# A decoder layer on one core: sums of squares moved from VectorE to adding DMAs, a named table set for Gelu, a new order on every engine

## The reference

```
re, im  = num_re / den, num_im / den
mean_sq = (sum(re**2) + sum(im**2)) / (2 * H * M)      # over the 8 x 4 values of a head
rs      = rsqrt(mean_sq + 1e-5)
y       = (re * rs * norm_re) @ W_re + (im * rs * norm_im) @ W_im
out     = (y * silu(gate)) @ out_proj
```

## Time and profile before

| | us |
|---|---|
| median of 3 runs | 1030.68 (1026.15 to 1031.63) |
| the profiled execution, own time | 1032.04 |
| its span, first to last instruction | 1030.3 |
| busy TensorE, VectorE, ScalarE, GpSimd | 911.1, 792.5, 565.7, 44.7 |
| mean granted TensorE clock | 0.963 of full speed |

### The profile page before, as it was taken

The page is one execution under the profiler, slowest core; times in us unless marked ns, Lnnn a source line. Parts: engine busy times, 40 slices in busy tenths (PEclk is TensorE's granted clock), DMA queues, the critical chain, the costliest instruction groups (busy, mean ns, idle before and its releaser), DMA issues.

```text
span 1030.3 us, 11040 instructions
## 1 busy us (share of the span) xinstructions
PE 911.1 (88%) x3719; PEld 553.9 (54%) x3738; DVE 792.5 (77%) x1301; ACT 565.7 (55%) x902; POOL 44.7 (4%) x112
## 2 busy tenths in 40 slices
PE   0489945889999999989998999989999999999795
PEld 0145623555575647654766457644766476647345
DVE  3778799778987899779987799779988997183141
ACT  0566674487428564767457553885467745421410
POOL 0000100100001000100010000100010002000000
PEclk9889986999999999999998999999999999999899
DMA  5900100010002000110001000200002000000000
GB/s 153 239 1 1 62 0 0 21 42 1 1 14 69 1 1 1 43 41 1 1 21 61 1 1 1 83 1 0 1 1 62 1 1 21 1 0 1 21 1 21
DMA packets 39082, 25.48 MB, mean 25 GB/s; under 512 B 18647, under 2 KB 38642, under 8 KB 39026
## 3 DMA queue, kind: packets, MB, share of 16 engines
q1 hardware_dynamic: 39026, 24.77, 8.6%
HBM read 20.57 MB, written 4.19 MB: 24 GB/s over the span
## 4 chain that ended last, share of the span: by engine, by line
PE 64%; DVE 15%; ACT 13%; issue 5%; SPq 1%; POOL 1%; DMA 0%; ACTq 0%; DVEq 0%; POOLq 0%
PE ps L811 9%; PE ps L792 9%; PE ps L783 9%; PE ps L672 7%; PE ps L610 4%; PE ps L595 3%; PE ps L640 3%; PE ps L716 3%; PE ps L463 3%; PE ps L656 3%; DVE zc L2460 2%; PE ps L726 2%; DVE sc L2539 2%; ACT x L1674 2%; ACT L1422 1%
## 5 line engine op out<-in xcount | busy, mean ns | idle before, releaser
L2539 DVE TENSOR_TENSOR_SCAN sc<-mask,sc 128x1024 f32<-128x1024 bf16 x64 | 146.3, 2285 | 0.5
L783 PE MATMUL ps<-cum,mw 128*128 128x512 f32 x256 | 121.9, 598 | 3.2 <-ACT cs L1669 2.9
L792 PE MATMUL ps<-x2t,mv 128*128 128x512 f32 x256 | 121.6, 597 | 1.6 <-DVE prod L2767 0.7
L811 PE MATMUL ps<-up,prod 128*128 128x256 f32 x512 | 116.2, 380 | 1.3 <-DVE prod L2767 0.9
L811 PEld LDWEIGHTS ps<-up,prod 128*128 128x128 f32 x512 | 95.1, 190 | 15.9 <-issue 3.8
L1669 ACT ACTIVATE cs<-ps 128x512 f32<-128x512 f32 x64 | 37.9, 592 | 102.4 <-PE ps L783 98.1
L2460 DVE SCALAR_TENSOR_TENSOR zc<-ps,cw,zc 128x510 f32<-128x510 f32 (+2 forms) x96 | 71.3, 743 | 22.7 <-ACT zc L1484 20.3
L2531 DVE TENSOR_TENSOR sc<-sc,g 128x1024 f32<-128x1024 f32 x64 | 77.7, 1214 | 9.7 <-ACT sc L1555 9.6
L1573 ACT ACTIVATE sq<-sc 128x1024 f32<-128x1024 f32 x48 | 50.4, 1050 | 58.7 <-DVE acc L2551 58.7
L783 PEld LDWEIGHTS ps<-cum,mw 128*128 128x128 f32 x256 | 47.3, 190 | 58.8 <-issue 56.2
L595 PE MATMUL ps<-xt,win 128*128 128x512 f32 x128 | 66.7, 650 | 9.5 <-DVE zc L2460 9.5
(11 more groups left out here) (263 smaller groups left out, 1551.6 us busy)
## 6 DMA issues: line engine op xcount, KB each, us to landing
xa<-in_x_dram SPq DMA_DIRECT2D x8, 512.0 KB, 3.5
xs_a<-in_x_dram SPq DMA_DIRECT2D x8, 512.0 KB, 3.8
cin<-in_ctx_dram SPq DMA_DIRECT2D x8, 512.0 KB, 5.6
out_dram<-prod SPq DMA_DIRECT2D x8, 512.0 KB, 4.8
prod<-in_L_ffn_V_fwd_dram SPq DMA_DIRECT2D x2, 256.0 KB
prod<-in_L_ffn_W_fwd_dram SPq DMA_DIRECT2D x2, 256.0 KB
prod<-in_L_ffn_W_inv_exp_dram SPq DMA_DIRECT2D x2, 256.0 KB
prod<-in_L_ffn_V_inv_dram SPq DMA_DIRECT2D x2, 256.0 KB
```

What stands on the lines that cost most here:

```text
L783: last = mm(o, mw[:, t, br, c:c + P], cum[:, t, :], start=(t == 0), stop=(t == 1))
L792: last = mm(o, mv[:, t, br, c:c + P], x2t[:, t, :], start=(t == 0), stop=(t == 1))
L811: mm(d, prod[:, j, q * P:(q + 1) * P], up[:, j, :], start=(j == 0), stop=False)
L2539: V.tensor_tensor_scan(flat, mask[:, 0:2 * T], flat, 0.0, ALU.mult, ALU.add)\
```

## The change

1. a_accumulate leaves VectorE. GpSimd issues a DMA with an adding destination in its place, 6 per chunk, 48 in all, each 128x1024 floats from sq[h] to acc[h], counted by a semaphore for each half. VectorE keeps the two half sums (a_both) and waits there for the third add of its half. ScalarE's squares wait for the DMA before, where they waited for VectorE's add.
2. c_hidden asks for a third set, GELU. ScalarE's list has 54 changes of set now.
3. The lists of all engines and of SP are new. biases() stands behind a_scan(0, 7) instead of ahead of a_moments(0, 2); the split of the bias row on GpSimd (bias_parts) stands behind rstd of b(0). At the end of a chunk VectorE does the residuals of b(i-1) and c(i-2) mostly between a_scan(i, 7) and a_both(i, .). In VectorE's list of the middle chunks the products of c stand ahead of units 2 to 7 of a. PE has b_transform(i, "cf") between a_squares(i) and its two a_factor, and transposes of c between those of a.

```diff
-EXP_LN, SILU_SIN = "natural_log_exp_and_others", "silu_and_others"
+EXP_LN, SILU_SIN, GELU = "natural_log_exp_and_others", "silu_and_others", "gelu_and_others"
...
+        added = [sem(f"pool_a_add{h}") for h in range(2)]
...
             load_x(1)
+            load_ctx(1)
+            load_residual(1)
             load_x(2)
-            load_residual(1)
-            load_ctx(1)
             load_x(3)
             load_residual(2)
             load_ctx(2)
+            store(0)
+            load_residual(3)
             load_x(4)
-            load_residual(3)
-            store(0)
             load_ctx(3)
+            load_ctx(4)
+            store(1)
+            load_residual(4)
             load_x(5)
...
# ScalarE, a_squares
-                    if m > 1:
-                        act.wait_ge(*VEC_A.at(i, "acc", u - 2))
-                    elif not is_first(i):
-                        act.wait_ge(*VEC_A.at(i - 1, "acc", UNITS - 2 + h))
+                    if m > 1 or not is_first(i):
+                        act.wait_ge(added[h], 16 * ((M - 1) * i + m - 1))
...
             def c_hidden(i, n):
-                tables(SILU_SIN)
+                tables(GELU)
...
# GpSimd
+            def a_accumulate(i, u):
+                m, h = divmod(u, 2)
+                pool.wait_ge(*ACT_A.at(i, "sq", u))
+                if m > 1:
+                    pool.wait_ge(added[h], 16 * ((M - 1) * i + m - 1))
+                else:
+                    pool.wait_ge(*ACT_A.at(i, "sq", h))
+                G.dma_start(acc[:, h, :, :], sq[:, h, :, :], accum_op=ALU.add).then_inc(added[h], 16)
+            a_accumulate(0, 2)
...
+            a_accumulate(0, 7)
             rstd(0, 0, VEC_A, POOL_A)
...
             rstd(0, 1, VEC_B, POOL_B)
+            bias_parts()
...
# VectorE
-            def a_accumulate(i, u):
-                m, h = divmod(u, 2)
-                dve.wait_ge(*ACT_A.at(i, "sq", u))
...
-                TT(acc[:, h, :, :], acc[:, h, :, :], sq[:, h, :, :], ALU.add).then_inc(*VEC_A.tick("acc", u))
-                if m == M - 1:
-                    dve.wait_ge(*VEC_A.at(i, "acc", u))
-                    TT(acc[:, h, 0, :], acc[:, h, 0, :], acc[:, h, 1, :], ALU.add).then_inc(*VEC_A.tick("both", h))
+            def a_both(i, h):
+                dve.wait_ge(added[h], 16 * (M - 1) * (i + 1))
+                TT(acc[:, h, 0, :], acc[:, h, 0, :], acc[:, h, 1, :], ALU.add).then_inc(*VEC_A.tick("both", h))
...
# VectorE's list, end of chunk 0 and of chunk 1
-            biases()
             a_moments(0, 2)
...
             a_scan(0, 7)
-            a_accumulate(0, 5)
-            a_accumulate(0, 6)
-            a_accumulate(0, 7)
+            biases()
+            a_both(0, 0)
+            a_both(0, 1)
             a_weight(0)
...
             a_scan(1, 7)
-            a_accumulate(1, 5)
-            a_accumulate(1, 6)
-            a_accumulate(1, 7)
+            b_residual(0, 0)
+            b_residual(0, 1)
+            a_both(1, 0)
+            a_both(1, 1)
             a_weight(1)
-            b_residual(0, 0)
             a_factor(1)
             a_heads(1, 0)
             a_heads(1, 1)
-            b_residual(0, 1)
             a_residual(1, 0)
```

More of the change, by code:

```diff
@@ L95 @@
               + each("p2 g both gf y", range(2)) + each("frac mom scan", range(UNITS))
-              + [("acc", u) for u in range(2, UNITS)] + LAYER_NORM)
+              + [] + LAYER_NORM)
 ACT_A = Steps("act_a", each("xT silu p1", range(2)) + ["zs", "exp", "phigh", "e", "ln", "f", "fhigh"]
@@ L823, in _ @@
             a_project(0, 2)
+            fold(0)
             a_project(0, 3)
-            fold(0)
+            a_sums(0, 0)
             fold(1)
@@ L871, in _ @@
             a_project(1, 0)
+            fold(33)
             a_project(1, 1)
@@ L926, in _ @@
             c_turn(0)
+            a_spread(2, 1)
+            a_project(2, 2)
+            c_own(0, 0)
+            b_spectrum(1, "qa")
+            b_spectrum(1, "qb")
+            b_spectrum(1, "ka")
+            b_spectrum(1, "kb")
+            b_spectrum(1, "va")
+            b_spectrum(1, "vb")
+            c_weights(0)
             a_project(2, 3)
[L928 to L931, removed]
             c_spread(0, 0)
@@ L1731, in _ @@
             a_angles(0, 4)
+            fold(11)
+            fold(12)
             a_turns(0, 6)
@@ L2309, in _, with bias_parts @@
                 G.memset(t, 0.0).then_inc(zeroed, 1)
-            pool.wait_ge(ready, 2)
-            pool.wait_ge(folded, len(FOLD))
-            for n in range(PARTS):
-                if n:
-                    pool.wait_ge(parts, 2 * n - 1)
-                    G.tensor_tensor(bp[:, :], bp[:, :], bp3[:, n - 1, :], ALU.subtract).then_inc(parts, 1)
-                    pool.wait_ge(parts, 2 * n)
-                G.tensor_copy(bp3[:, n, :], bp[:, :]).then_inc(parts, 1)
+            def bias_parts():
+                pool.wait_ge(ready, 2)
+                pool.wait_ge(folded, len(FOLD))
+                for n in range(PARTS):
+                    if n:
+                        pool.wait_ge(parts, 2 * n - 1)
+                        G.tensor_tensor(bp[:, :], bp[:, :], bp3[:, n - 1, :], ALU.subtract).then_inc(parts, 1)
+                        pool.wait_ge(parts, 2 * n)
+                    G.tensor_copy(bp3[:, n, :], bp[:, :]).then_inc(parts, 1)
             @staged
@@ L2335, in _ @@
             rstd(2, 0, VEC_A, POOL_A)
+            a_accumulate(3, 2)
+            a_accumulate(3, 3)
+            a_accumulate(3, 4)
+            a_accumulate(3, 5)
+            a_accumulate(3, 6)
+            a_accumulate(3, 7)
+            rstd(2, 1, VEC_B, POOL_B)
             rstd(1, 2, VEC_C, POOL_C)
-            rstd(2, 1, VEC_B, POOL_B)
             rstd(3, 0, VEC_A, POOL_A)
+            a_accumulate(4, 2)
+            a_accumulate(4, 3)
+            a_accumulate(4, 4)
+            a_accumulate(4, 5)
+            a_accumulate(4, 6)
+            a_accumulate(4, 7)
+            rstd(3, 1, VEC_B, POOL_B)
             rstd(2, 2, VEC_C, POOL_C)
-            rstd(3, 1, VEC_B, POOL_B)
             rstd(4, 0, VEC_A, POOL_A)
+            a_accumulate(5, 2)
+            a_accumulate(5, 3)
+            a_accumulate(5, 4)
+            a_accumulate(5, 5)
+            a_accumulate(5, 6)
+            a_accumulate(5, 7)
             rstd(3, 2, VEC_C, POOL_C)
@@ L2895, in _ @@
             a_fraction(2, 3)
+            c_normalise(0)
             a_scan(2, 1)
             a_conv(2, 2)
-            c_softmax(0)
-            c_normalise(0)
             c_split(0)
-            a_conv(2, 3)
+            b_products(1)
             c_scale(0, 0)
             c_prod(0, 0)
+            b_heads(1)
+            c_scale(0, 1)
+            c_prod(0, 1)
+            b_topk(1)
+            b_weight(1)
+            c_scale(0, 2)
+            c_prod(0, 2)
+            c_scale(0, 3)
+            a_conv(2, 3)
+            c_prod(0, 3)
+            c_scale(0, 4)
+            b_apply(1)
+            c_prod(0, 4)
+            b_mix(1)
+            c_scale(0, 5)
+            c_prod(0, 5)
             a_moments(2, 2)
             a_fraction(2, 4)
-            c_scale(0, 1)
             a_scan(2, 2)
```

1096 lines of the change are left out of this document (532 added, 564 removed).

## The result

The kernel after takes 995.12 us (median of 4 runs, 994.89 to 1000.13) against 1028.81 (4 runs, 1026.15 to 1031.63): a ratio of 0.9684, 95% interval 0.9640 to 0.9727, 33 us. The span of the profiled execution fell from 1030.3 to 993.5. The forecast was 1014, the range began at 1004: the direction was right, the size was not.

A forecast was written before the change was run, and what follows sets the result against it. TensorE was taken to set the pace from 225 to 950 us, its work fixed, so only its idle time could shrink. 1030.3 - 3 - 4 - 10 = 1013.3 of span, say 1014 measured; own range 1004 to 1022, whole range to 1042.

The forecast's parts named there:

- D = 5.9: Time of one adding DMA: 3.5 us plus half again for the second read, plus 0.6 for GpSimd's issue.
- from chunk 2 on D costs nothing: Ends of chunks from 2 on: the add's transfer is hidden, cost nothing; if cover is gone, 3.5 us a chunk.
- The rival of long adds: Adds longer than two scans hold up ScalarE's squares, deciding from 8.5 us; 1050 at 10 us; chance 0.20.
- Chunk 0, -3: End of chunk 0: bias work behind the last scan hides the add, three adds leave; -3 us, between 0 and -4.
- Chunk 1, -4: End of chunk 1: earlier last scan, normaliser near 183.2 against 188.20, residual work ahead; -4 us, between 0 and -9.
- The steady stretch, -10: 225 to 950 us: half of TensorE's waits on ScalarE and VectorE go, less 1.5 new waits; -10, between +5 and -20.
- Tables: ScalarE: 11 fewer table loads, 14.1 us; rival that this fails loses the ScalarE half, 7.3: 1021, chance 0.08.
- SP's and GpSimd's queues: Reordered loads, stores and normaliser steps: costed at nothing; at worst 3.5 us once for SP, 1 us a chunk for GpSimd.
- PE's floor: Rival: steady stretch already at 96.5%, waits only move; only chunks 0 and 1 give, some 4 us: 1028; chance 0.18.
- Ports: Rival: each GpSimd issue holds VectorE 0.2 to 1.0 us, only the tables help: 1026 to 1031, say 1028; chance 0.06.

The follow-up runs named there:

- e14: Kernel after with all 48 adds left out (no VectorE add, no DMA): 996.21 us, ratio 0.9670 to the kernel before.
- e12: Kernel after with one small GpSimd instruction ahead of each add DMA: 1026.96 us, ratio 0.9980 to the kernel before.
- e18: Kernel after with biases() back ahead of unit 2's moments on VectorE: 995.99 us, ratio 0.9669 to the kernel before.
- e13: Kernel before's old order with Gelu's own table and all 48 adds left out (no VectorE add, no DMA): 1019.02 us, ratio 0.9891 to before.
- e1: Kernel before with one edit, c_hidden asking for the Gelu table set: 1024.08 us, ratio 0.994 to before.
- e5: Kernel before with the adds as DMAs and Gelu's own table, in the old order of TensorE, ScalarE and VectorE: 1029.59 us, ratio 1.0003 to before.
- e8: Kernel after with two serial small GpSimd instructions ahead of every add DMA: 1060.38 us, ratio 1.0304 to the kernel before.
- e2: Kernel before in its old order with only the 48 adds moved to DMAs from GpSimd: 1034.33 us, ratio 1.0045 to before.
- e10: Kernel after with SP's loads and stores and two places of GpSimd's normaliser steps in the old order: 996.18 us, ratio 0.9682 to the kernel before.
- e4: Kernel after with the 48 adds back on VectorE, each chunk's last two right ahead of the half sums: 1049.61 us, ratio 1.019 to the kernel before.
- splices: Adds as DMAs, Gelu's table; old order to chunk 4's squares, then new: 1021.32 us; new order to chunk 1's squares, then old: 1024.44 us.

## Why the prediction was wrong

**The adds, D = 5.9.** Measured 4.9 from square to landing (4.6 from the issue's start), nearer the row of 3.5 us, as chosen; GpSimd's 0.86 us at the issue lies within the 4.6. I let 0.6 for it come on top. No run shows the half again that I added for the second read. The term "from chunk 2 on D costs nothing" was right for the new order (e14), and for the right reason only in part: TensorE is busy until then.

**The rival of long adds.** Its mechanism is real, its point was wrong. I counted 28.7 us of room and a start at 8.5; at 6.9 the cost is already 4.0 us a chunk (e12). The error, as I see it, is in the sum: TensorE's lag of 8.0 us and VectorE's lead of 7.2 were added to the scans' 14.9 as if free, but the half sums that end a chunk must be there when TensorE comes, and that lag is what the last transfer uses. My own rows said so: 7.0 + 1.4 = 8.4 against 8.0. Had D been 6.9, 1.0 above my figure and 2.0 above the measured one, the time would have been 1027. So the forecast was nearer to a failure than its 0.20 says; that D came out on the good side was in part luck.

**Chunk 0, -3.** Measured -0.4 at the squares (98.02 to 97.58), and that with three folds left to do behind them. The reason fell as well: the bias move hides nothing (e18). It could not have hidden the add by my own figures: the last add lands 7.0 us after the scan, and biases() takes 5.0.

**Chunk 1, -4.** The squares come 4.3 us earlier in all, and one context transform (16 matmuls, 3.7 us) is done ahead of them besides: about 8 for the two terms' 7. The place was right: idle PE between chunks 0 and 1 is put to use.

**The steady stretch, -10: the step that failed.** Measured -31.5 between the squares of chunks 1 and 7. The prediction said "PE's work is the same before and after, so the span can only shrink by idle PE time", and gave back "half of each" of the waits, because engines were relieved. The runs show this in its place:
- What relief gives was sized about right. With the adds gone altogether in the old order (e13) this stretch takes 664.9 us against 672.3 before, 7.4 less, most of it the tables' (e1: 665.2); the whole kernel gains 11 us. Of the whole time nothing is left once the transfers have to be waited for (e5). TensorE's largest waits stand in all these runs where they were (rows of 3.3, 3.2 and 2.3 us, as before).
- The reorder was the missing term. Without any adds it takes the stretch from 664.9 us (e13) to 641.6 (e14), 23.3 us less, of which 3.7 are a context transform that it does ahead of the stretch, and it covers the transfers besides (after: 640.9). In the prediction it had no term of its own in the steady stretch; it stood there only as one extra matmul. The waits that I had halved for the relief went because of the order.
- The order removed most of the idle time: PE's idle between these milestones is 28.9 before and 9.1 after. Some 4 of the 28.9 (an estimate) are 15 matmuls whose records are missing (L800, 33 of 48): e5, where none is missing, has 24.8.
- TensorE's busy time is not fixed. It fell by 11.7 us between the milestones, and by 12.6 from e5 to after. 3.7 are the context transform done earlier. Some 6 (an estimate) are matmuls at the lower clock: before, TensorE was busy at a granted clock of 0.50 for some 12 us of this stretch, near 194, 225 and 562 us; after, no 5 us of it have a clock below 1.00. What makes the rest is not shown. The slow ones show in one group, of the interval of chunk 5, before and after:

```profile
L672 PE MATMUL ps<-wks,spec 128*128 128x256 f32 x16 | 6.8, 585 | 3.2 <-ACT qkv L1604 3.2
```
```profile
L673 PE MATMUL ps<-wks,spec 128*128 128x256 f32 x16 | 4.0, 385 | 0.2 <-ACT qkv L1603 0.2
```

Busy time of before in the 5 us behind that wait, the clock in the third place from the end:

```profile
560.00:565.00 5.00, 5.00 (x14) 4.03 (x13) 4.93 (x5) 1.49 (x3) 0.00 (x0) 0.50 0.00 0
```

A wait of 3.2 us cost 2.8 more in this group (6.8 us, where it takes 4.0), at a granted clock of 0.50, the lower of TensorE's two levels (1.2 GHz). In e8 the interval grew by 47.0 us over after: 34.2 are idle, 12.8 are busy time.

**Tables.** 54 loads, as walked; worth 6.4 alone, 4.2 in the new order, 4.7 beside the adds (e2 to e5), against a half credit of 7.3 for ScalarE. The mechanism holds: this relief did reach TensorE. It is the smallest part.

**SP's and GpSimd's queues**, costed at nothing: right (e10).

**The other rivals.** PE's floor (1028) is near e5, the old order (1029.6), but in the number only: there chunks 0 and 1 give nothing (squares of chunk 1 at 188.8, 187.1 before), and in after it is the steady stretch that gives. Ports: VectorE's scans take 2284 ns (2285 before) and its moments 1207 (1214), so the issues took nothing from it.
The Trainium skill (page SBUF — State Buffer, section Who interferes with whom) has VectorE and GpSimd share a pair of ports under a lock. The lock did not show between issue and VectorE, but GpSimd's own small instructions grew beside VectorE (below).

**What stays open:** which engine's list carries the 23 us that the order gains without any adds, and which chunk; splices could not say it within their own losses. Which moves of the order remove TensorE's waits is therefore not shown either, only that the order does.

## What to carry to other kernels

Relief on engines that do not set the pace is worth little by itself (11 us for some 64 taken off VectorE and ScalarE, e13) and nothing when a new wait comes with it (e5), and an order made for the relief can be worth less than nothing without it (e4): cost the two together, and give the reorder its own term, since it can take nearly all of the idle time of the engine that sets the pace. Count a TensorE wait of some microseconds at more than its length. Before moving an accumulation to a DMA, compare square plus landing, in series, with the spacing of its producers, and be sure of the margin: 2.0 us more on each transfer, on the average, took nearly the whole gain (e12).

## What the hardware showed that I had not expected

- An adding DMA of 512 KB from SBUF to SBUF, issued by GpSimd, lands 4.6 us after the issue starts (4.5 to 6.2 over 48), 0.86 us of it GpSimd's. By the fit in the Trainium skill (page DMA: Bandwidth & Descriptors, section Anatomy of one DMA) a plain copy would take 3.2 us, an estimate that no run here shows; the measured add took 1.4 more.
- The same small GpSimd instruction takes 1.01 us at the normalisers and, beside VectorE's products and scans, 1.42 (e8) or 1.70 us (e12) on the average, up to 5.4. The DMA issue stays at 0.87 to 0.92 on the average, at most 1.37.
- After TensorE had stood 3.2 us, the granted clock was 0.50 for over 5 us (559 to 565 in before), and 16 matmuls took 585 ns instead of 385 each. After a like wait at 672 us in e5 it stayed at 1.00.
